# Six and two head pairs in the two halves of the output projection, in place of four and four, in a local-attention stack on one core

## The reference

```python
for i in range(6):
    x = attn_layer(shift_tokens(x), Wqkv[i], q_scale[i], k_scale[i], Wo[i]) + x
    x = ffn_layer(shift_tokens(x), ln_g[i], ln_b[i], W1[i], b1[i], W2[i], b2[i]) + x

def attn_layer(x, Wqkv, qs, ksc, Wo):
    q, k, v = split(x @ Wqkv)               # 16 heads of 64
    q = rotary(l2norm(q) * qs); k = rotary(l2norm(k) * ksc)
    out = local_attention(q, k, v)          # windows of 32, each sees itself and the one before
    return out.reshape(b, n, 1024) @ Wo     # the output projection

def ffn_layer(x, g, bln, W1, b1, W2, b2):
    xn = layernorm(x) * g + bln
    a, gate = split(xn @ W1 + b1)
    return a * gelu(gate) @ W2 + b2
```

## Time and profile before

| what | us |
|---|---|
| median of 3 runs | 3821.89 |
| lowest and highest of them | 3813.36 and 3839.02 |
| the profiled execution's own time | 3819.22 |
| its span, from the first to the last instruction | 3817.4 |
| of that the slots of the block in question, from and to | 581 to 2310 |

### The profile page before, as it was taken

The page is one execution under the profiler, slowest core; times in us unless marked ns, Lnnn a source line. Parts: engine busy times, 40 slices in busy tenths (PEclk is TensorE's granted clock), DMA queues, the critical chain, the costliest instruction groups (busy, mean ns, idle before and its releaser), DMA issues. The chain is left out here.

```text
span 3817.4 us, 124590 instructions
## 1 busy us (share of the span) xinstructions
PE 3211.2 (84%) x53825; PEld 2471.0 (65%) x53825; DVE 2587.7 (68%) x4478; ACT 1957.8 (51%) x3747; POOL 1720.2 (45%) x1651
## 2 busy tenths in 40 slices
PE   6675948999999999999999996798989886866557
PEld 2223537888888888888888884476767675422235
DVE  6996457777777777777777773655555534699713
ACT  5552225666666666666666662344444432355223
POOL 1662016665666565666566562232222221066542
PEclk9887969999999999999999996678887886899778
DMA  1000011111101111111111110000000000000121
GB/s 44 1 1 19 0 36 50 41 30 45 41 27 46 41 30 45 41 28 48 39 30 28 28 30 8 4 6 7 7 7 7 6 5 7 8 1 1 68 59 47
DMA packets 72473, 96.86 MB, mean 25 GB/s; under 512 B 14678, under 2 KB 48244, under 8 KB 70788
## 3 DMA queue, kind: packets, MB, share of 16 engines
q1 hardware_dynamic: 69668, 84.74, 7.5%
q0 software_dynamic: 2272, 4.27, 0.3%
HBM read 35.60 MB, written 8.40 MB: 12 GB/s over the span
## 5 line engine op out<-in xcount | busy, mean ns | idle before, releaser
L2212 POOL TENSOR_TENSOR local_rot<-local_term 128x512 f32<-128x512 f32 x384 | 479.5, 1270 | 647.4 <-DVE local_term L2566 647.4
L2566 DVE TENSOR_TENSOR local_term<-bank,local_table 128x512 f32<-128x512 f32 x768 | 488.1, 683 | 258.2 <-ACT local_sq L2444 256.5
L278 POOL TENSOR_TENSOR mamba_hc<-mamba_state,mamba_c_all 128x512 f32<-128x512 f32 x256 | 325.8, 1294 | 253.4 <-DVE mamba_state L502 238.2
L2220 POOL TENSOR_TENSOR local_rot<-local_rot,local_inv 128x512 f32<-128x512 f32 x384 | 397.5, 1057 | 30.3 <-ACT local_inv L2455 29.8
L2245 PE MATMUL bank<-local_w_layer,local_xs 128*128 128x256 f32 x1536 | 387.8, 395 | 8.7 <-issue 4.2
L2245 PEld LDWEIGHTS bank<-local_w_layer,local_xs 128*128 128x128 f32 x1536 | 277.9, 191 | 49.6 <-issue 6.5
L339 PE MATMUL bank<-mamba_hc,ident 128*128 128x512 f32 x512 | 266.1, 645 | 24.0 <-DVEq L511 18.3
L2255 PE MATMUL bank<-local_w_layer,local_xs 128*128 128x128 f32 x1536 | 216.8, 284 | 26.4 <-ACT local_pt L2471 26.4
L2444 ACT ACTIVATE local_sq<-bank 128x512 f32<-128x512 f32 x384 | 219.9, 591 | 36.4 <-PE bank L2245 33.3
L2578 DVE TENSOR_REDUCE local_sums_q<-local_sq 128x8 f32<-128x512 f32 x384 | 235.6, 655 | 0.0
L2287 PEld LDWEIGHTS bank<-local_k_rot,local_q_rot 64*32 64x32 f32 x12288 | 180.5, 107 | 84.4 <-issue 84.4
(11 more groups left out here) (456 smaller groups left out, 7926.0 us busy)
## 6 DMA issues: line engine op xcount, KB each, us to landing
local_v_moved<-local_v_at SPq DMA_DIRECT2D x192, 198.0 KB, 2.5
local_w_layer<-a_w_layer_dram SPq DMA_DIRECT2D x6, 1536.0 KB, 7.1
local_v_moved<-local_v_at SPq DMA_DIRECT2D x192, 33.0 KB, 2.9
routed_w<-f_w_dram SPq DMA_DIRECT2D x3, 2048.0 KB, 16.7
local_w_o<-a_w_o_dram SPq DMA_DIRECT2D x6, 512.0 KB
rows_dram<-fresh SPq DMA_DIRECT2D x1, 2574.0 KB, 11.9
routed_x_in<-rows_dram SPq DMA_DIRECT2D x13, 198.0 KB, 5.6
routed_y_in<-y_dram SPq DMA_DIRECT2D x8, 256.0 KB, 4.9
```

The lines of the kernel that those rows point to most:

```text
L278: ins = pool.tensor_tensor(hc[:, n % 2, h, :], state[:, n % 2, h, :], c_all[:, n % 2, :], ALU.mult)
L2212: pool.tensor_tensor(rot[:, s % 2, :, f, :], here[:, :, f, :], there[:, :, 1 - f, :], ALU.add).then_inc(summed, 1)
L2220: pool.tensor_tensor(one, one, spread(inv[:, s % 2, heads], E), ALU.mult).then_inc(normalized, 1)
L2566: dve.tensor_tensor(term[:, which, b, :], g.bank[b][:, :], table[:, which, :, :].rearrange("p n c -> p (n c)"), ALU.mult).then_inc(roped, 1)
```

## The change

Six of the eight head pairs are taken in the first half of the output projection and two in the second. Nothing else is edited; `some.stop`, used in the wait at line 2324, becomes 6 in place of 4 for the first half and stays 8 for the second.

```diff
@@ local_stack
         ROUNDS = CHUNKS * HALVES
+        FIRST_PAIRS = 6
@@ project_out
             def project_out(f, half):
-                l, some = f // GROUPS, range(PAIRS // 2 * half, PAIRS // 2 * (half + 1))
+                l, some = f // GROUPS, range(FIRST_PAIRS, PAIRS) if half else range(FIRST_PAIRS)
                 if half == 0:
                     if f % GROUPS == 0:
                         pe.wait_ge(ffn_loaded, 64 * (l + 1))
                     pe.wait_ge(up_copied, ROUNDS * f) if f else None
                 pe.wait_ge(o_copied, PAIRS * f + some.stop)
```

## The result

The changed kernel has a median of 3798.36 us over 21 runs (3784.67 to 3808.31), the kernel before, run beside it, 3822.51 us over 21 (3806.76 to 3839.02). The ratio is 0.9925 with a 95% interval of 0.9913 to 0.9937, which is 29 us less (24 to 33); the two medians by themselves are 24.2 us apart, at the lower end of that. The forecast was 30.5 us, 0.992. The profiled execution took 3792.69 us, 26.5 us less than that of before and 4.0 us more than the 3788.7 that the sum gave for it.

A forecast was written before the change was run, and what follows sets the result against it. TensorE was taken to bound the block, with ScalarE setting the k = 0 slots. 30.0 us there and 0.5 at the end, pauses taken as nothing, made 30.5 off the median's 3821.9: 3791.4 us, range 3778 to 3811.

The forecast's parts named there:

- What bounds it: Block: TensorE bounds it, but ScalarE sets the 22 k = 0 slots with GELUs, which costs 30.0 us, 1.36 a slot.
- The price of a pair: Output projection on TensorE: four head pairs take 3.57 us, so one is 0.89 us and the two moved are 1.785.
- The wait for six copied pairs: Head of the projection's first half: costs nothing, since `weigh_values(s - 2)` ahead of it already waits for the same number.
- The k = 0 slots: The 22 slots with GELUs: the wait at line 2255 goes entirely and each lasts 11.88 us, 0.21 to 0.63 longer.
- The margin of 0.2 us in the worst slot: k = 0 slot with the longest wait: TensorE would allow the copy at 2246.37, still 0.2 us behind ScalarE.
- The k = 1 slots and the chain behind them: Each falls from 10.09 to 8.31 us; VectorE's and GpSimd's work up to the next slot's `turn_heads` keeps 1.1 us spare.
- the third rival: GpSimd's line 2220 after k = 1 does not come sooner; 4 us given back, 3795 us in all; chance 0.08.
- The end of the block: Behind the last slot: the second half starts later but is 1.785 us shorter, so it ends 0.5 us sooner.
- The pauses: TensorE's "issue" time without a named wait, 19.0 us in 23 pauses: may shift by 19.0 us either way, taken as nothing.
- the fourth rival: TensorE's "issue" pauses shift: 3772 us at one end, 3810 at the other; sign: over 5 us moved; chance 0.08.
- The shared bank: k = 0 slots: `V_BANK`, serving probabilities and values, makes the copy follow the transposes; 13.24 us slots, 3821 in all; chance 0.06.
- The slower side: k = 1 slots: GpSimd's and VectorE's chain holds them at 10.09 us, giving 3832 in all; chance 0.04.

## Why the prediction was right, point by point

- **What bounds it.** TensorE, with 30.0 us in the k = 0 slots set by ScalarE. Confirmed from two sides: with the table loads gone the wait is gone in the even split, and with one pair less moved (five) ScalarE sets the slots at the same lengths. The prediction says "because of the GELUs"; without their two table loads, equally long work in their place made no wait. Of the 23 waits that the prediction looked for in these slots, 22 lay there, with 26.0 us by the idle column, so that the modelled ends hide 4.0 of the 30.0 us, 0.18 a slot.
- **The price of a pair.** 0.89 us: six pairs now take 720.27 - 714.92 = 5.35, which is 6 x 0.89.
- **The wait for six copied pairs.** It costs nothing; TensorE has no idle time ahead of line 2328 in the k = 0 slots, and none there with seven pairs either, whose slots last the 12.77 us of their matmuls.
- **The k = 0 slots.** 11.88 forecast, 11.87 to 11.88 measured. The margin of 0.2 us in the worst slot was 0.20, that of 0.63 in the slot of the example 0.64. The margin tells that the sixth pair was needed and a seventh not.
- **The k = 1 slots and the chain behind them.** 8.31 forecast, 8.30 measured outside pauses; 1.1 us left before line 2272, measured 1.12. The norms came sooner with line 2256, as the prediction had it, so the third rival, with its 4 us given back, is out.
- **The end of the block.** 0.5 us forecast. In the profiled execution after the change the lower clock behind a pause hides it (line 2296 took 1.06 us in place of 0.60), and the end of the block took 2.0 us more than before. The second profile of the changed kernel has the full clock there. From the start of the first half to the end of the second it takes 2290.49 - 2281.13 = 9.36 us, where it took 2317.87 - 2308.01 = 9.86 before: 0.50 us less, as forecast. First the first half before, then both halves in the second profile:

```profile
2308.01 3.73 PE L2327 MATMUL bank<-local_w_o,local_attn 128*128 128x128 f32 x32
```

```profile
2281.13 5.52 PE L2328 MATMUL bank<-local_w_o,local_attn 128*128 128x128 f32 x48
2288.44 2.05 PE L2328 MATMUL bank<-local_w_o,local_attn 128*128 128x128 f32 x16 [0.72 <-ACT local_attn L2477]
```

- **The pauses.** Taken as nothing, which was too little. Their sum indeed stayed (19.0, then 20.3 and 19.4), so that the sign of the fourth rival, a move by more than 5 us, did not come; that they shift "against the transfers" no run shows. But outside the 44 slots, the block's slots took 3.4 us more than before in the first profile and 2.7 in the second. With the 2.5 us by which the end missed its forecast in the first profile, and 1.9 us less in the rest of the program, that is the 4.0 us by which the profiled execution missed the sum. A pause costs more where the clock falls behind it. One slot with k = 3 had lasted 10.06 us at the full clock; after, a pause of 1.26 us fell into it, and the clock with it:

```profile
2236.03:2249.32 13.29, 11.88 (x183) 10.15 (x183) 6.84 (x12) 6.26 (x14) 5.24 (x6) 0.87 0.07 20
```

```profile
2240.17 0.30 PE L2309 MATMUL last_banks<-local_pt,local_v_at 64*64 64x32 f32 x4 [1.26 <-issue]
2240.41 3.65 PE L2246 MATMUL bank<-local_w_layer,local_xs 128*128 128x256 f32 x8
```

  Line 2246 took 3.65 us where it takes 1.99 to 2.00 at the full clock, and the slot 3.2 us more than before. The change did not bring this in: the kernel before had such a slot too, at another place (k = 6, a pause of 1.27 us), so the clock was not quite "full throughout":

```profile
1852.98:1864.42 11.44, 10.17 (x166) 8.42 (x165) 7.87 (x16) 5.10 (x11) 6.26 (x6) 0.85 0.20 69
```

- **The size.** By the medians 3791.4 us was forecast and 3798.4 measured. Of the 7.0 us, 4.0 are the ones above; the other 3.0 come from the step from one execution to a median, as the profiled one of the changed kernel lies 5.7 us under its median and not 2.7.
- **The rivals.** The shared bank is out (46.3 us of waits with three and five, and 0.4 us in the even split without table loads). By the Trainium skill, page "Perfetto Trace Analysis", section "Optimization Strategy", a repeating gap can mean too few buffers; here it vanished with the buffers unchanged. The slower side, a chain that holds the k = 1 slot above 9.67 us, is out at 8.30 and even at 7.40.

## What to carry to other kernels

Where the bounding engine waits for another only in some slots of a repeating pattern, movable work of that engine belongs into those slots, ahead of what waits; compare the slot with the wait to a like one without it, and the difference is the gain and says how much to move. Move until the margin of the late engine turns positive in the worst slot; more is neither gain nor loss as long as the slot that was relieved has a chain short enough. And look at the queue of waits already passed before pricing a new one: a wait for a number that an earlier instruction has waited for is free.

## What the runs showed of the hardware that was not expected

A wait on TensorE can cost more than its length. With waits of 1.0 to 1.4 us by the idle column ahead of line 2255 (four pairs), none of the k = 0 slots or the ones behind lost the full clock. With the wait 0.89 us longer (three pairs, 1.9 to 2.3 us) the granted clock fell to 0.50 behind it in 11 of 22 groups, at some 16 us in all (35.6 us more in the 44 slots, of which 22 x 0.89 = 19.6 are the moved pairs), and with 0.89 us more again (2.8 to 3.2 us) during it or behind it in 17 of 22. Filling the wait with repeated transposes brought the full clock back in these slots of all 22 groups.

The length of the wait alone does not decide. With three pairs, waits of 1.87 us lost the full clock in three groups, and waits of 2.27 to 2.29 us kept it in four. Pauses of 1.26 and 1.27 us lost it (after and before), and pauses of 1.81 and 1.82 us kept it (seven pairs, and the changed kernel's second profile). What decides was not tried.

The pauses named "issue" return in the same slots when the same program runs again, and partly in others when the program's order is changed. The Trainium skill, page "Runtime: NRT & Kernel Launch", section "Instruction fetch mechanics", says that instructions are streamed in blocks and that crossing a block's boundary is mostly hidden; pauses that stick to a place in the program would fit such a boundary that is not hidden, but no run here shows what they are.
